# Four moves in a deformable-convolution kernel: first clamp, transpose stores, one input load, and the distances of a chunk

## The chip, the cores and the metric

The kernel runs on one core of a Trainium2 chip. Its engines are TensorE (PE), VectorE (DVE), ScalarE (ACT), GpSimd (POOL) and SyncE (SP), which each work through their own list of instructions and wait for each other by semaphores. The metric is the device time in microseconds (us); the time before is 4453.39 us, the median of three runs (4452.77 to 4454.16).

## What is computed

The input `x` is 8 images of 32 channels and 64 by 64 pixels in float32. It is normalised per image and channel, goes through four blocks and a final layer, and the result is added to `x`:

```python
def _block(x, dc_w, dc_b, of_w, of_b, dw, db):
    h = relu(_deconv2d(x, dc_w, dc_b))           # 3x3
    offset = _conv2d(h, of_w, of_b, PAD)         # 3x3, 18 offsets for each pixel
    return relu(_deform_conv2d(h, offset, dw, db))
in_module = x                                    # the normalised input
x = _block(x, ...0); in_prev = 0
for i in range(1, 4):
    in_cur = x + in_prev
    x = _block(in_cur, ...i)
    in_prev = in_cur
x_cat = concatenate((x, in_module), axis=1)      # 64 channels
offset = _conv2d(x_cat, fin_off_w, fin_off_b, PAD)
return _deform_conv2d(x_cat, offset, fin_dcn_w, fin_dcn_b)
```

`_deform_conv2d` reads each of the 9 taps of a pixel at a place moved by its offsets, with bilinear weights between the four neighbours.

## The kernel before

**Steps.** The work is 5 layers times 2 groups of 4 images, in order: 10 steps, which this text numbers 0 to 9. Steps 0 to 7 belong to the four blocks (a loop `Fori(0, LAYERS)` with both groups in its body), steps 8 and 9 to the final layer. A step has a head and a sampling part. All engines meet at barriers (`clear_step`, `sampling`) between them.

**The head of a step (steps 0 to 7).** PE convolves the input in two units of 32 rows (`conv_tiles`, L516); ACT and DVE write the result to `H` (L828, L994). PE transposes `H` (L531), ACT copies the transposes to the staging tiles `A` (unit 0) and `VT` (unit 1) (`keep_transposes`, L813), and SP stores them to `ht_store` in DRAM (`store_ht`, L371), five DMAs for each unit. PE convolves `H` to the offsets (L516 again). DVE takes them in 8 items of 512 columns: one pass to `FOFF` (L1012) and two reductions for maximum and minimum (L1015, L1016). SP stores each item with two DMAs (`store_offsets`, L379). When the four items of unit 0 have landed, SP loads the offsets of the first two chunks back into `HB`, spread over partitions (`load_offsets`, L389, eight DMAs for each chunk). ACT makes the distances of chunk 0 (`distance`, L730, `DIST`), DVE clamps them (`clamp`, L900), and POOL splits them into two halves of float16, the hats (`hats`: a cast, L1076, then a subtraction, L1078, to `HL`). In the program of DVE the clamp of chunk 0 stands before item 4; in that of POOL `hats(0, 0)` stands before the all-reduce. After item 7 DVE reduces the ranges over columns (to L1035), POOL takes the maximum over partitions (`partition_all_reduce`, L1092), and DVE works out the flags (L1040 to L1062) that choose the shape of the sampling. Then the barrier.

**The sampling.** Each step has 32 chunks of 128 pixels for each of 4 images. The chosen shape is `Shape(0, ...)` (windows of 11 by 11) in steps 0 to 7, and `Shape(1, 2)` (windows of 16 by 16, two batches for each chunk) in steps 8 and 9, as the shapes of the instructions in the trace tell. A chunk has 12 groups g of weights for a batch. For each g PE spreads the y hats and the x hats to the window's positions (L545), ACT copies the y factor out of PSUM (`YC`, L761), and DVE multiplies both to `A` (`one_product`, L895). PE multiplies `A` with the window `VT` (`sample`, L563) for the chunk before in three parts, after g = 4, 7 and 10; ACT reads each part (L740). After g = 1 PE sums the chunk two back over taps (`deform`, L576), ACT reads that (L723) and DVE adds it to the image after product 3 (L889). The y slots in PSUM number 3 and the x slots 4: the spread of y for g waits for the copy of g - 3, that of x for the product of g - 4.

**What the next chunk needs.** While chunk c is worked on, ACT makes the distances of chunk c + 1 (`next_distance`) and DVE clamps them; then POOL makes the hats. Where they stand is set by `next_after`: in shape 0 the distances follow copy 1 and the clamp follows product 2. In shape 1 both follow g = 4 and 5 of the first batch. SP loads the offsets of chunk c + 2 and the windows of chunk c + 1 (L389, L397) in its own loop. The chunk loop (`chunk_loop`) runs two chunks in each of 14 turns, with two chunks in front of it and two behind.

**The final layer** has no first convolution. It needs the normalised input again: SP loads it to `H` at the layer's start (`load_normal(0)`, L354), DVE normalises it (L1001), and PE transposes `X` first and `H` when that is done. Its second group's load is issued in step 8's sampling. `later_loads` also bring the plain input back to `X`.

## Time and profile before

| | us |
|---|---|
| median of three runs | 4453.39 |
| the profiled execution, its own time | 4450.75 |
| its span, first to last instruction | 4448.9 |
| PE busy in it | 3883.5 |
| DVE busy | 3017.8 |
| ACT busy | 2803.3 |
| POOL busy | 1140.5 |
| mean granted clock of TensorE | 0.938 of full speed |

The steps begin some 381 to 387 us apart in steps 0 to 7; steps 8 and 9 take longer. Each instruction stands in the trace with its start and its length. "Idle before" is the time that the engine had nothing to do before it, and behind the arrow stands what ended it; "issue" is idle time that ended without a semaphore that the profile shows. A row of the timeline can hold several instructions in a row (x3); its length is then that of all. PEq, SPq, POOLq and ACTq are the engines' sequencers, which wait, branch, compute addresses and issue DMAs.

### The profile page before, as it was taken

The numbers are of one execution on the slowest core, as the hardware profiler recorded it, in microseconds if no ns is written. First come the engines' busy times: TensorE is split into PE (matmuls) and PEld (weight loads), VectorE is DVE, ScalarE is ACT, GpSimd is POOL, SyncE is SP. The second block draws the span as 40 slices with busy tenths as digits, with TensorE's granted clock in tenths as the row PEclk, the third lists the DMA queues.
The fourth block names the chain that finished last, engine by engine and source line by source line (L and its number), as shares of the span: only waits on it lengthen the run. The fifth ranks groups of instructions, "written<-read, shape, count | busy, mean of one in ns | idle before, by whom it ended". The sixth has DMA issues, their size and how long they took to land.

```text
span 4448.9 us, 221697 instructions
## 1 busy us (share of the span) xinstructions
PE 3883.5 (87%) x81888; PEld 2914.2 (66%) x81888; DVE 3017.8 (68%) x5838; ACT 2803.3 (63%) x6651; POOL 1140.5 (26%) x655
## 2 busy tenths in 40 slices
PE   4998799599879969987986997798699999799998
PEld 3676576477657647765764775576577777577776
DVE  4786588388568738856874884786377776377775
ACT  2786488288558828856873884687155555255554
POOL 0332243033123303413331341332011221012211
PEclk8999899799989979998997998899799999899999
DMA  3442443244244334424433442443666664666664
GB/s 116 122 120 64 122 121 109 75 119 121 62 124 121 102 81 120 122 59 127 120 92 91 121 121 64 121 120 100 172 159 150 150 153 108 170 153 149 153 155 109
DMA packets 243252, 527.18 MB, mean 118 GB/s; under 512 B 61152, under 2 KB 151776, under 8 KB 225632
## 3 DMA queue, kind: packets, MB, share of 16 engines
q1 hardware_dynamic: 242880, 522.27, 45.2%
q8 instruction: 227, 3.72, 0.4%
q14 instruction: 145, 1.19, 0.1%
HBM read 465.57 MB, written 56.45 MB: 117 GB/s over the span
## 4 chain that ended last, share of the span: by engine, by line
PE 49%; issue 17%; DVE 14%; ACT 9%; DMA 3%; SPq 2%; DVEq 2%; ACTq 2%; POOL 1%; POOLq 1%; PEld 0%; PEldq 0%
PE P L545 19%; PE PS L563 19%; DVE A L895 11%; PE P L516 6%; ACT YC L761 5%; PE PS L576 4%; ACT DIST L730 3%; SPq L389 1%; ACT H L828 1%; POOL HL L1078 1%; DMA X<-x_dram 1%; DVEq L927 1%; PE PS L516 1%; DMA HB<-off_store 1%; DVE DIST L900 1%
## 5 line engine op out<-in xcount | busy, mean ns | idle before, releaser
L895 DVE TENSOR_TENSOR A<-P,YC 121x384 f32<-121x384 f32 (+1 forms) x4608 | 2300.1, 549 | 843.5 <-ACT YC L761 627.3
L545 PE MATMUL P<-HL,SEL 32*121 32x384 f16 (+1 forms) x21504 | 1759.7, 304 | 356.7 <-issue 202.2
L761 ACT ACTIVATE YC<-P 121x384 f32<-121x384 f32 (+1 forms) x4608 | 1719.0, 444 | 288.2 <-PE P L545 249.5
L545 PEld LDWEIGHTS P<-HL,SEL 32*121 32x121 f16 (+1 forms) x21504 | 1076.9, 116 | 807.7 <-issue 400.1
L563 PE MATMUL PS<-A,VT 121*32 121x80 f32 (+1 forms) x40960 | 1331.5, 248 | 44.1 <-ACT SMP L740 15.3
L563 PEld LDWEIGHTS PS<-A,VT 121*32 121x32 f32 (+1 forms) x40960 | 1083.3, 116 | 352.8 <-issue 176.5
L1076 POOL CAST HL<-DIST 128x1152 f16<-128x1152 f32 x320 | 366.2, 1144 | 3065.9 <-DVE DIST L900 3065.9
L740 ACT ACTIVATE SMP<-PS 128x480 f32<-128x480 f32 (+3 forms) x1152 | 593.7, 515 | 687.8 <-PE PS L563 682.6
L1078 POOL TENSOR_TENSOR HL<-DIST,HL 128x1152 f16<-128x1152 f32 x320 | 765.9, 2393 | 133.5 <-issue 74.3
L576 PE MATMUL PS<-SMP,CW 128*64 128x128 f32 x7424 | 475.9, 277 | 5.4 <-ACT SMP L740 5.4
L730 ACT ACTIVATE DIST<-HB,CONST 128x1152 f32<-128x1152 f32 x320 | 403.1, 1260 | 103.7 <-DMA HB<-off_store 101.9
L576 PEld LDWEIGHTS PS<-SMP,CW 128*64 128x64 f32 x7424 | 398.7, 137 | 86.6 <-issue 72.5
L889 DVE SCALAR_TENSOR_TENSOR X<-X,CONST,TMP 128x128 f32 (+1 forms) x320 | 280.4, 876 | 79.7 <-ACT TMP L723 79.7
L900 DVE TENSOR_SCALAR DIST<-DIST 128x1152 f32<-128x1152 f32 x320 | 240.2, 751 | 99.1 <-ACT DIST L730 99.1
L516 PE MATMUL P<-X,W 32*32 32x512 f32 x5040 | 208.9, 663 | 89.9 <-POOLq L255 58.2
L516 PEld LDWEIGHTS P<-X,W 32*32 32x32 f32 x5040 | 132.1, 107 | 139.7 <-issue 112.4
L723 ACT ACTIVATE TMP<-PS,BIAS 128x128 f32<-128x128 f32 x320 | 119.0, 372 | 150.2 <-PE PS L576 149.7
L828 ACT ACTIVATE H<-P,BIAS 32x512 f32<-32x512 f32 x128 | 87.8, 686 | 192.5 <-PE P L516 160.6
L516 PE MATMUL P<-H,W 32*32 32x512 f32 x5040 | 207.7, 636 | 1.1 <-issue 1.1
L516 PEld LDWEIGHTS P<-H,W 32*32 32x32 f32 x5040 | 137.6, 105 | 56.5 <-issue 23.1
L994 DVE TENSOR_SCALAR H<-P,BIAS 32x512 f32<-32x512 f32 x96 | 72.0, 750 | 145.2 <-PE P L516 117.8
L1012 DVE SCALAR_TENSOR_TENSOR FOFF<-P,PXB 128x512 f32<-128x512 f32 x70 | 47.8, 683 | 156.6 <-PE PS L516 99.2
(56 smaller groups left out, 667.3 us busy)
## 6 DMA issues: line engine op xcount, KB each, us to landing
HB<-off_store SPq DMA_DIRECT2D x2560, 72.0 KB, 2.4
VT<-ht_store SPq DMA_DIRECT2D x256, 512.0 KB
VT<-ht_store SPq DMA_DIRECT2D x768, 132.0 KB
VT<-ht_store SPq DMA_DIRECT2D x256, 88.0 KB
off_store<-FOFF SPq DMA_DIRECT2D x160, 128.0 KB, 2.6
ht_store<-A SPq DMA_DIRECT2D x32, 256.0 KB, 3.4
ht_store<-VT SPq DMA_DIRECT2D x32, 256.0 KB, 3.6
A<-x_dram SPq DMA_DIRECT2D x2, 2048.0 KB, 10.4
```

Source lines behind the costliest of these rows:

```text
L516: mm = nc.tensor.matmul(bank(bank0 + i)[CH * j:CH * (j + 1), :], weights[q, CH * k:CH * (k + 1)], view(row + k // 3 - 1, col + k % 3 - 1)[ ...
L545: mm = nc.tensor.matmul(dst, SEL[q, table, 0:sh.npos], hats, start=part == 0, stop=part == 1)
L563: mm = nc.tensor.matmul(PS[q:q + wide, sh.unit * v:sh.unit * (v + 1)].rearrange("p (k y x) -> p k y x", k=sh.taps, y=BLK), vt[:, img, :], ...
L576: mm = nc.tensor.matmul(PS[64 * pair:64 * (pair + 1), 0:CPX], CW[:, 64 * k:64 * (k + 1)], rhs, start=k == 0, stop=k == sh.taps - 1)
L730: nc.scalar.activation(DIST[:, :], HB[:, half, :], ACT.Abs, bias=HAT_BIAS).then_inc(abs_done, 1)
L740: nc.scalar.activation(smp_px(0, sh, b * sh.blocks + w, s, count), PS[:, 0:sh.unit * count], ACT.Copy).then_inc(ps_free, 1)
L761: nc.scalar.activation(YC[0:sh.npos, g % X_SLOTS, 0:sh.size], P[0:sh.npos, g % Y_SLOTS, 0:sh.size], ACT.Copy).then_inc(y_ready, 1)
L889: return nc.vector.scalar_tensor_tensor(dst, dst, flag, src, ALU.mult, ALU.add)
L895: return nc.vector.tensor_tensor(dst, x, y, ALU.mult)
L900: nc.vector.tensor_scalar(DIST[:, :], DIST[:, :], SCALE, SCALE, ALU.min, ALU.subtract).then_inc(clamp_done, 1)
L1076: nc.gpsimd.tensor_copy(HL[:, 0, half, :], DIST[:, :]).then_inc(hat_step, 1)
L1078: nc.gpsimd.tensor_tensor(HL[:, 1, half, :], DIST[:, :], HL[:, 0, half, :], ALU.subtract).then_inc(hats_full, 1)
```

## The change

1. **DVE** does the clamp of chunk 0 after the ranges' last operation (L1035), where it waits for the all-reduce, and no longer before item 4.
2. **POOL** does the all-reduce first and the hats of chunk 0 after it.
3. **The stores of the transposes** are issued by ACT, in steps 0 to 7 after each unit's five copies and in steps 8 and 9 after all twenty.
4. **SP** loads the offsets of chunk 0 after unit 0 as before, but those of chunk 1 after all eight items are stored.
5. **The final layer's input** for group 0 is loaded to `H` in the sampling of each block's second group (steps 1, 3, 5 and 7), with a wait for it at the end of SP's sampling; the load at the final layer's start is gone. The first three of the four loads are overwritten by the next layer.
6. **In shape 0** the distances of chunk c + 1 stand in front of copy 0 of chunk c, not behind copy 1, and its clamp stands behind product 1, not product 2. Shape 1 stays as it was.

```diff
-        self.next_after = self.sum_after if self.batches == 1 else self.after[0]
+        self.next_at = 0 if kind == 0 else self.after[0]
@@ SP
                 if final:
-                    load_normal(0)
                     sp.dma_start(CW[:, :], t["fin_dcn_w"]).then_inc(sum_loaded, 16)
@@ SP, step
                 for unit in range(UNITS):
-                    for half in range(UNITS) if final and unit == 0 else [] if final else [unit]:
-                        for n in range(BANKFULS):
-                            store_ht(sources, half, n)
                     for n in range(IMG * unit, IMG * (unit + 1)):
                         store_offsets(n)
                     if unit == 0:
                         for slot in range(OFF_SLOTS):
                             sp.wait_ge(off_stored[slot], 32)
                         load_offsets(0, 0)
-                        load_offsets(0, 1)
+                load_offsets(0, 1)
...
                     if not final and group == GROUPS - 1:
                         load_conv(layer + 1)
+                        load_normal(0)
+                def finish():
+                    if not final and group == GROUPS - 1:
+                        wait_alone(sp, final_loaded, 16 * (layer + 1))
@@ ACT, body
                             n = (c * sh.batches + b) * sh.ngr + g
+                            if sh.kind == 0 and g == sh.next_at and not last:
+                                next_distance(c + 1, band + half, 1 - half)
                             act.wait_ge(y_full, n + 1)
                             act.wait_ge(product_done, n + 1)
                             nc.scalar.activation(YC...).then_inc(y_ready, 1)
-                            if b == 0 and g == sh.next_after and not last:
+                            if sh.kind > 0 and b == 0 and g == sh.next_at and not last:
                                 next_distance(c + 1, band + half, 1 - half)
@@ ACT, step
+                def store_ht(unit, n):
+                    sources = 2 if final else 1
+                    first, count = sheet(unit, n)
+                    width = sources * 128
+                    act.wait_ge(ht_copied, (UNITS * (sources - 1) + unit) * BANKFULS + n + 1)
+                    ...
+                    act.dma_start(dst, staged(sources, unit, n, count)...).then_inc(ht_stored, 16)
...
                     for unit in range(UNITS):
                         keep_transposes(0, unit)
+                        for n in range(BANKFULS):
+                            store_ht(unit, n)
@@ DVE
-                            if b == 0 and g == sh.next_after + 1 and not last:
+                            if b == 0 and g == sh.next_at + 1 and not last:
                                 clamp(c + 1)
...
-                    dve.wait_ge(final_loaded, 16 * (group + 1))
+                    dve.wait_ge(final_loaded, 16 * (LAYERS + group))
...
-                    if n == IMG:
-                        clamp(0)
...
                 flag_count[0] += 1
+                clamp(0)
                 chained()
@@ POOL, step
-                hats(0, 0)
                 pool.wait_ge(flag_step, 4)
                 nc.gpsimd.partition_all_reduce(...).then_inc(flag_step, 1)
+                hats(0, 0)
```

## Rows read from the trace of the kernel before

**Rows 1.** Waits in total: engine line <- what ended them: us, times, longest.

```profile
POOL HL L1078 <- issue: 74.3, 10, 7.9
POOL ST L1092 <- issue: 59.8, 10, 6.7
```

**Rows 2.** Timeline of DVE, head of step 0: start, length, line, idle before.

```profile
90.79 0.76 DVE L900 TENSOR_SCALAR DIST<-DIST 128x1152 f32<-128x1152 f32 x1 [10.16 <-ACT DIST L730]
...
99.69 0.16 DVE L1035 TENSOR_TENSOR ST<-ST,CONST 128x4 f32<-128x4 f32 x1
...
104.29 0.16 DVE L1062 SCALAR_TENSOR_TENSOR FLAG<-ST 128x1 int32<-128x1 f32 x1
```

**Rows 3.** Timeline of PE, step 0: offset convolution's end, chunk 0, chunk 1.

```profile
79.39 3.00 PE L516 MATMUL P<-H,W 32*32 32x512 f32 x68
...
105.79 8.42 PE L545 MATMUL P<-HL,SEL 32*121 32x384 f16 x48 [20.85 <-issue]
121.41 3.65 PE L545 MATMUL P<-HL,SEL 32*121 32x384 f16 x20 [7.21 <-POOL HL L1078]
```

**Rows 4.** Timeline of SP's DMA issues, step 0.

```profile
83.11 7.30 SPq L389 DMA_DIRECT2D HB<-off_store  x16
90.46 3.29 SPq L371 DMA_DIRECT2D ht_store<-VT  x5
93.79 5.76 SPq L379 DMA_DIRECT2D off_store<-FOFF  x8
107.60 9.02 SPq L397 DMA_DIRECT2D VT<-ht_store  x8
116.66 11.97 SPq L389 DMA_DIRECT2D HB<-off_store  x24
```

**Rows 5.** Timeline of POOL, step 0: all-reduce, then chunk 1's subtraction.

```profile
101.79 0.39 POOL L1092 PARTITION_ALL_REDUCE ST<-ST  x1 [6.04 <-issue]
...
118.92 2.35 POOL L1078 TENSOR_TENSOR HL<-DIST,HL 128x1152 f16<-128x1152 f32 x1 [6.95 <-issue]
```

**Rows 6.** Timeline of ACT, step 0: the distances of chunk 2.

```profile
123.38 1.25 ACT L730 ACTIVATE DIST<-HB,CONST 128x1152 f32<-128x1152 f32 x1
```

**Rows 7.** Timeline of SP's DMA issues, step 7.

```profile
2769.47 7.38 SPq L389 DMA_DIRECT2D HB<-off_store  x16
...
2793.57 8.88 SPq L397 DMA_DIRECT2D VT<-ht_store  x8
```

**Rows 8.** Timeline of ACT, step 0: the distances of three later chunks.

```profile
232.04 1.27 ACT L730 ACTIVATE DIST<-HB,CONST 128x1152 f32<-128x1152 f32 x1
...
241.09 1.26 ACT L730 ACTIVATE DIST<-HB,CONST 128x1152 f32<-128x1152 f32 x1
...
250.01 1.27 ACT L730 ACTIVATE DIST<-HB,CONST 128x1152 f32<-128x1152 f32 x1
```

**Rows 9.** Timeline of DVE, a steady chunk: product 2.

```profile
144.12 0.56 DVE L895 TENSOR_TENSOR A<-P,YC 121x384 f32<-121x384 f32 x1 [1.06 <-ACT YC L761]
```

**Rows 10.** Timeline of PE, the same chunk: the x spread of g = 7.

```profile
145.86 0.53 PE L545 MATMUL P<-HL,SEL 32*121 32x384 f16 x2 [0.27 <-DVE A L895]
```

**Rows 11.** Chain of work across the loop's turn: start, us, what.

```profile
149.98 0.04 ACT YC L761
...
150.50 0.06 ACT YC L761
...
150.78 0.04 ACTq L251
...
151.10 0.05 ACTq L251
```

**Rows 12.** Timeline of PE, step 8: the first transposes of H.

```profile
3118.23 1.10 PE L531 MATMUL P<-IDENT,H 128*128 128x128 f32 x4 [8.80 <-DVE H L1001]
```

**Rows 13.** DMA issues of the page: xcount, KB each, median us to landing.

```profile
HB<-off_store SPq DMA_DIRECT2D x2560, 72.0 KB, 2.4
...
H<-x_dram SPq DMA_DIRECT2D x2, 2048.0 KB, 19.4
```

## What I predict

> **What bounds the kernel now.** I read the waits first, then the timelines of one step's head, engine by engine, then the chain across a steady chunk. There are three stretches with different limits.
>
> The **head of steps 0 to 7** is a chain with little overlap. PE ends the offset convolutions at 79.39 + 3.00 = 82.39 [rows 3], so item 4 could be taken then. DVE stands idle for 10.16 us instead, because its next instruction is the clamp of chunk 0, which begins at 90.79 when ACT's distances are done [rows 2]; these need the offsets of chunk 0, whose loads begin at 83.11 [rows 4]. Item 4 follows at about 91.5, the ranges end at 99.69 + 0.16 = 99.85, the flags at 104.45 [rows 2]. PE begins chunk 0 at 105.79 after 20.85 us of idleness, works 8.42 us, and then waits 7.21 us for the hats of chunk 1 [rows 3]: their subtraction starts only 6.95 us after the cast, an idle time that nothing released [rows 5]. This stands in all ten steps (74.3 us in ten waits), as does a similar one before each all-reduce (59.8 us in ten) [rows 1]. I read both as POOL fetching the code of the other function each time that it changes between them.
>
> The **steady chunks of shape 0** take 8.92 us, and 9.05 us across a turn of the loop: the distances start at 232.04, 241.09 and 250.01 [rows 8]. No engine is full. DVE waits 1.06 us for copy 2 [rows 9], which stands behind the distances on ACT, and PE waits 0.27 us for product 3 before its x spread of g = 7 [rows 10]. The ring is: last copy, distances, copy, product 3, spread, part, read of the part, last copy.
>
> **Steps 8 and 9** are bound by PE and keep their chunk loop. Step 8's head has PE waiting 8.80 us for the normalised input [rows 12].
>
> **The sum, part by part**, against the profiled 4450.75 us (2.64 below the median; I add that difference at the end).
>
> *Head of steps 0 to 7.* Without the clamp in front, item 4 starts at 82.4 and the ranges end 99.85 - 9.1 = 90.8 in step 0. The clamp then lies beside the all-reduce (0.76 us against at least 0.39). ACT's five stores of unit 1 cost what SP's did, 3.29 us [rows 4], after copies that follow PE's 82.4 at once; the distances behind them wait for the offsets anyway (83.11 + 3.65 + 2.4 = 89.2 [rows 4, 13]). That cover is nearly used up, and if a store costs more there, the distances and the clamp are late by as much.
>
> Next is late what SP has to do. Its list after 83.11 is eight loads (half of 7.30 = 3.65), eight stores (5.76), and then the eight loads of chunk 1 (3.65), which now stand behind the stores [rows 4]. It comes to the barrier at 83.11 + 3.65 + 5.76 + 3.65 + 0.1 = 96.3. The flags end 104.45 - 101.79 = 2.66 us after the all-reduce's start [rows 2, 5], which I put 0.1 to 1.9 us behind the ranges (the latter as now): at 93.6 to 95.4. So **SP is last at the barrier**. From the flags' end to the first window load it was 107.60 - 104.45 = 3.15 us; so the windows begin at 99.4, which is 8.2 us earlier. The same sum in step 7 gives 24.10 - 16.4 = 7.7 us [rows 7]. I take 8.0 for each of the eight.
>
> Does chunk 1 follow? On POOL the order is now all-reduce, cast, code, subtraction. With the all-reduce's code fetched while POOL idles, it ends at 91.3 to 93.1. To this come cast and gaps (an estimate, 1.6: the cast is the lighter half of the hats), code 7.0, subtraction 2.4 [rows 5] = 11.0 us, against 105.79 - 102.18 = 3.6 us before: the fetch is not gone, it moves from chunk 1 to chunk 0. Chunk 0 starts at 102.3 to 104.1; PE's 8.4 us of it [rows 3] cover the hats of chunk 1, whose subtraction needs no fetch now. So chunk 1 could start at 110.7 to 112.5. Its ACT work begins with the distances of chunk 2, and their offsets land at 116.66 - 8.2 + 3.7 + 2.4 = 114.6 [rows 4, 13]. They start there, 8.7 us before the old 123.38 [rows 6]. Copies 0 and 1 then stand behind them and not in front, some 0.8 us, so copy 2 is 8.0 us early. POOL's path has 2 us to spare. **Eight heads: -64 us**, bounds -52 (a store on ACT at twice its cost, 1.5 us each) and -74 (9.1 us for each, the whole of DVE's gain).
>
> *Steady chunks, steps 0 to 7.* Between the last copy of a chunk and product 3 of the next, ACT and DVE do the same work in either order; only the idle time of DVE moves from product 2 to product 0. I take that at 0 to -0.08 us. But in front of copy 0 stand the sequencer's instructions. Before the distances ACT computes two semaphore values and waits twice: from 150.78 to 151.10 + 0.05 that is 0.37 us [rows 11], now hidden under copies 0 and 1. Across the turn copy 0 starts 150.50 - 149.98 = 0.52 us after the last copy [rows 11], and the 0.13 us more of such a chunk [rows 8] show that this start is in the ring and that within a turn a copy takes 0.39 us. In the new order those 0.39 us cover the sequencer within a turn; across the turn the branch has used that cover already. The distances would start 0.37 us later than that, and all behind them. So 14 turns x 8 steps x (0.37 - 0.09) = +31 us, and -5 us for the other 120 chunks: **+26 us**. Bounds: -19 us, if the sequencer gets ahead (232 chunks x -0.08), and +60 us, if product 0's delay also reaches the part after g = 4.
>
> *Step 8.* DVE has nothing else to do before the input comes, and PE is free 8.80 us before its transposes of H [rows 12]: **-8.8 us**. Those transposes' DMA stores follow on ACT long before anything needs them.
>
> *Steps 8 and 9.* Item 4 waits for PE there, so the clamp gives 0 to -0.6 us. SP comes to the barrier with eight more loads, +0.6 us each; chunk 0's later hats lie under the wait for the input that comes back to X. **+1 us.**
>
> *The four input loads.* 2 MB each, behind the offsets of chunk 3. The two such loads of before took 19.4 us in the median, one of them behind another 2 MB [rows 13]. The next offsets in the queue are needed two chunks later, 18 us. I take **+1 us** in all, bounds 0 and +12 (3 us each). SP's wait for them at the end of the 32 chunks costs nothing.
>
> Sum: -64 + 26 - 8.8 + 1 + 1 = -44.8; profiled 4406, median **4408 us**.
>
> **The rivals.**
> - *The loop does not pay.* The sequencer gets ahead of the branch, or the 0.08 us show. For it: one instruction is usually in the engine's queue ahead. Against it: the 0.13 us of the turn were not hidden. 4408 - 26 - 10 = 4372 us (4360 to 4385).
> - *The all-reduce fetches its code when it is called, not when POOL comes to it.* In this kernel the mechanism would be 6 us behind the ranges instead of the 1.94 us of step 0 (101.79 - 99.85). Chunk 1 would start at 97.2 + 11 + 8.4 = 116.6, two us later than by SP's queue; with the final steps' flags 4 us late that is 8 x 2.5 + 8 = 28 us more: 4436 us. Against it: the all-reduce began 1.94 us after its input was there, so 6 us had not been spent since. The Trainium skill says in GPSIMD Engine Reference, section 2.1, that the first call to a freshly loaded kernel pays some 6 us of loading with no instruction in the profile; by that the reload moves with the first call, and the trace agrees on its size (59.8 / 10) but leaves open when it starts.
> - *Slower: the late product 0 stalls PE.* Product 0 now comes 1.06 us later in the chunk [rows 9], and the x spread of g = 4 and the part behind it wait for it. The part waited for the read of the sum behind the distances anyway, so I estimate that 0.4 us of it arrive there. PE has 0.27 us of idle time behind it [rows 10]. If the spread of g = 7 is pushed back, each 0.1 us costs 23 us; above 0.33 us for each chunk over what I have, it eats everything. With the full 0.4 us, 232 x 0.4 = 93: 4408 - 26 + 93 = 4475 us.
> - *Mixed*: ACT's stores or the loads cost their upper bounds, 4425 to 4440 us.
>
> **How the numbers follow.** Forecast (4390 to 4428) 0.56; no pay in the loop 0.22; mixed 0.09; code at the call 0.07; stall 0.06. The range for 8 in 10 takes in most of the second case and ends above the mixed one: 4368 to 4440. A measurement of this kernel can tell about 0.2% (9 us) from no change, so faster means below 4444.5: 0.89; within 0.2% 0.05; slower 0.06.
>
> **What would show it.** Item 4 at 9 us earlier after item 3, with the ranges' end; SP's eight loads behind the eight stores, and SP as the last at the barrier; the fetch of 7 us before chunk 0's subtraction and none before chunk 1's; the distances of chunk 2 released by their DMA; 9.3 us for a chunk across the loop's turn and 8.9 within it; DVE's idle time of 1 us before product 0; PE without a gap between its transposes of X and H. Wrong would make me: an all-reduce 6 us after the ranges, a DMA wait in chunks 4 and 5 of steps 1, 3, 5 and 7, or a chunk of over 9.3 us in both places.

## The result and the profile after

The changed kernel takes **4395.35 us** in the median of four runs (4392.15 to 4397.59), the kernel before 4453.08 us beside it (4450.37 to 4454.16): a ratio of **0.9871** (95% interval 0.9854 to 0.9888, as behind every ratio below), 57.7 us less. The forecast was 4408 us in a range of 4368 to 4440, so the time came out inside it. The working under it did not hold: its two largest terms were both wrong by over 50 us, and in opposite directions. The profiled execution took 4396.28 us (span 4394.4), 54.5 us less than that of before.

I cut both traces at the same instructions: the first offset item of a step (line 1024, before 1012), the distances of chunks 2, 3 and 31 (line 727, before 730), and the read of the last sum (line 720, before 723). The differences, after minus before, with what the forecast had:

| stretch | forecast, us | measured, us |
|---|---|---|
| heads of steps 0 to 7, first offset item to distances of chunk 3 | -64 | +0.6 |
| chunks 3 to 31 of steps 0 to 7, without the input loads (from e10, below) | +26 | -96.7 |
| the four input loads, in those chunks | +1 | +25.1 |
| between steps 7 and 8 | -8.8 | -10.4 |
| steps 8 and 9: heads +18.2, chunks +3.3 | +1 | +21.5 |
| what comes before the first cut, behind the last chunks, between the other steps | 0 | +5.4 |
| sum | -44.8 | -54.5 |

Up to the distances of chunk 2 the eight heads are 11.0 us shorter together (403.5 to 392.5), up to those of chunk 3 no longer (481.2 to 481.8). Part 6 itself moves these instructions within their chunk; e1, which has parts 1 to 5 without it, gives -6.3 and -0.2 us for the same two cuts.

**The head of step 0.** Timelines of the changed kernel, engine by engine: start, length, engine, line, operation, count, and in brackets the idle time before it with what ended it.

```profile
89.73 0.16 DVE L1047 TENSOR_TENSOR ST<-ST,CONST 128x4 f32<-128x4 f32 x1
...
94.92 0.16 DVE L1075 SCALAR_TENSOR_TENSOR FLAG<-ST 128x1 int32<-128x1 f32 x1
```

```profile
90.03 0.39 POOL L1104 PARTITION_ALL_REDUCE ST<-ST  x1 [84.98 <-DVE ST L1047]
92.26 1.14 POOL L1089 CAST HL<-DIST 128x1152 f16<-128x1152 f32 x1 [1.84 <-DVE DIST L914]
100.74 2.35 POOL L1091 TENSOR_TENSOR HL<-DIST,HL 128x1152 f16<-128x1152 f32 x1 [7.33 <-issue]
107.96 1.14 POOL L1089 CAST HL<-DIST 128x1152 f16<-128x1152 f32 x1 [4.87 <-DVE DIST L914]
109.28 2.37 POOL L1091 TENSOR_TENSOR HL<-DIST,HL 128x1152 f16<-128x1152 f32 x1 [0.18 <-POOL HL L1089]
```

POOL's sequencer at the all-reduce of step 0 (count, shortest/median/longest in ns, start of the first and the last):

```profile
L1104 POOLq MODIFY_POOL_CONFIG  x2: 11/11/11, 32.7 to 32.7; - x2
```

```profile
86.35 7.19 SPq L370 DMA_DIRECT2D off_store<-FOFF  x8
93.58 3.85 SPq L380 DMA_DIRECT2D HB<-off_store  x8
106.23 9.05 SPq L388 DMA_DIRECT2D VT<-ht_store  x8
```

```profile
104.45 9.05 PE L542 MATMUL P<-HL,SEL 32*121 32x384 f16 x60 [20.43 <-issue]
```

```profile
121.30 1.25 ACT L727 ACTIVATE DIST<-HB,CONST 128x1152 f32<-128x1152 f32 x1 [9.38 <-DMA HB<-off_store]
```

DVE has the ranges at 89.89 where it had them at 99.85 [rows 2], and the flags at 95.08. The all-reduce starts 0.14 us behind the ranges; its change of configuration stood at 32.7, long before its input. That the 7.33 us ahead of the subtraction are the loading of code is my reading: the trace shows the idle time and the change of configuration before it, not the loading itself. SP has issued its last load before the barrier at 97.43, and then issues nothing until 106.23; before, the windows began at 107.60 [rows 4]. PE starts chunk 0 at 104.45, where it was 105.79 [rows 3]. Of the 9.4 us gained at the flags, 1.3 arrive; and since this step began 0.8 us earlier (its first offset item at 72.08, before at 72.89), only 0.5 of them are the head's. The one engine that is busy in between is POOL: its subtraction for chunk 0 ends at 100.74 + 2.35 = 103.09, and PE follows 1.4 us later. SP's wait at the barrier (L253) ends at 103.19, and its first window follows after 3.0 us of its own reads and address work.

**The steady chunks.** First two groups of the page's part 5 (before, then after): busy us and mean ns, then the idle time ahead. It is the update of X by the sum of the chunk two back, which I call the residual; it stands on DVE behind product 3.

```profile
L889 DVE SCALAR_TENSOR_TENSOR X<-X,CONST,TMP 128x128 f32 (+1 forms) x320 | 280.4, 876 | 79.7 <-ACT TMP L723 79.7
```

```profile
L903 DVE SCALAR_TENSOR_TENSOR X<-X,CONST,TMP 128x128 f32 (+1 forms) x320 | 172.2, 538 | 79.7 <-ACT TMP L720 79.7
```

The same instruction on the same data is 338 ns shorter in the mean, 108 us in all. Beside it stands POOL's cast of the hats. DVE and POOL in one chunk of before, then in one of after:

```profile
226.66 1.08 DVE L889 SCALAR_TENSOR_TENSOR X<-X,CONST,TMP 128x128 f32 x1
```

```profile
226.44 1.14 POOL L1076 CAST HL<-DIST 128x1152 f16<-128x1152 f32 x1 [5.30 <-DVE DIST L900]
```

```profile
221.80 0.61 DVE L903 SCALAR_TENSOR_TENSOR X<-X,CONST,TMP 128x128 f32 x1
```

```profile
221.12 1.14 POOL L1089 CAST HL<-DIST 128x1152 f16<-128x1152 f32 x1 [4.97 <-DVE DIST L914]
```

Before, the cast begins 0.22 us ahead of the residual, ends at 227.58, and the residual at 227.74. After, the distances stand two copies earlier in ACT's list and the clamp one product earlier in DVE's, and the cast begins 0.68 us ahead of the residual; it ends at 222.26, the residual at 222.41. In both the residual ends 0.15 us behind the cast, however long it has run, and so it does in all 232 such chunks of each execution (0.14 to 0.16). A chunk takes 8.58 us in the mean of steps 0, 2, 4 and 6 (8.98 before), and its chain has only PE in it. The line of shares above the chain of waits of 203 to 230 us of after:

```profile
by line: PE P L542 54.2%; PE PS L560 32.8%; PE PS L573 13.8%
```

The turn of the loop costs 8.70 - 8.47 = 0.23 us, before 0.13 [rows 8].

**The input loads.** In steps 1, 3, 5 and 7 the mean chunk is 8.79 us and not 8.58. SP's issues in step 1 of after:

```profile
492.43 0.66 SPq L355 DMA_DIRECT2D H<-x_dram  x1
493.46 14.93 SPq L380 DMA_DIRECT2D HB<-off_store  x8
...
531.62 4.01 SPq L380 DMA_DIRECT2D HB<-off_store  x8
535.98 3.93 SPq L388 DMA_DIRECT2D VT<-ht_store  x4
540.57 3.84 SPq L380 DMA_DIRECT2D HB<-off_store  x8
544.79 3.95 SPq L388 DMA_DIRECT2D VT<-ht_store  x4
549.00 4.00 SPq L380 DMA_DIRECT2D HB<-off_store  x8
```

The eight small loads behind the 2 MB copy take 14.93 us to issue, against 4 us. Afterwards SP has no pause left: a turn of two chunks from 531.62 to 549.00 is 17.38 us of issuing one after the other, and PE would need 8.47 + 8.70 = 17.17, or 17.09 as in step 1 of e10. So the lost time isn't made up until the end of the step. In step 0 SP issues one after the other too, but its turn takes 222.59 - 205.49 = 17.10 us, a little less than PE's:

```profile
205.49 3.84 SPq L380 DMA_DIRECT2D HB<-off_store  x8
...
222.59 3.84 SPq L380 DMA_DIRECT2D HB<-off_store  x8
```

So in the even steps SP stays ahead; in the odd ones it lives on the lead it has at the start, which the copy takes away. Why its turn is longer there is open. The waits of after have, for PE's wait for windows (us, times, longest):

```profile
PE PS L560 <- DMA VT<-ht_store: 31.7, 49, 1.9
```

### The profile page after: what moved, and what is told of

Read it like the earlier page. It is cut to its first block, busy times and chain, and to the rows that moved or that the text cites. A ratio compares the mean times of both kernels' runs of the same rounds, so it can differ in the third digit from the quotient of the medians.

```text
span 4394.4 us, 221688 instructions
## 1 busy us (share of the span) xinstructions
PE 3849.4 (88%) x81888; PEld 2958.5 (67%) x81888; DVE 2931.0 (67%) x5838; ACT 2782.9 (63%) x6651; POOL 1145.0 (26%) x655
## 4 chain that ended last, share of the span: by engine, by line
PE 61%; SPq 21%; issue 7%; DMA 3%; POOLq 3%; ACT 2%; DVE 2%; POOL 0%; ACTq 0%; DVEq 0%; PEld 0%; PEldq 0%
PE P L542 22%; PE PS L560 22%; SPq L388 10%; SPq L380 10%; PE P L513 7%; PE PS L573 7%; POOLq L256 2%; ACT H L840 1%; PE PS L513 1%; DMA X<-x_dram 1%; DMA HB<-off_store 1%; PE P L528 1%; DVE FOFF L1024 1%; DMA off_store<-FOFF 0%; DVE ST L1028 0%
## 5 line engine op out<-in xcount | busy, mean ns | idle before, releaser
L542 PE MATMUL P<-HL,SEL 32*121 32x384 f16 (+1 forms) x21504 | 1730.0, 303 | 323.1 <-issue 216.2
L542 PEld LDWEIGHTS P<-HL,SEL 32*121 32x121 f16 (+1 forms) x21504 | 1124.0, 116 | 697.1 <-issue 351.6
L903 DVE SCALAR_TENSOR_TENSOR X<-X,CONST,TMP 128x128 f32 (+1 forms) x320 | 172.2, 538 | 79.7 <-ACT TMP L720 79.7
```

The costliest lines, as they stand in the source:

```text
L542: mm = nc.tensor.matmul(dst, SEL[q, table, 0:sh.npos], hats, start=part == 0, stop=part == 1)
```

## The experiments

My theories by then: **port**, that the residual is held while POOL's cast or subtraction runs, and the new order only moves it; **barrier**, that POOL's own arrival is last since its hats stand ahead of it; **loads**, that a copy on SP costs what SP can't make up. Their rival throughout is the prediction's own working.

### e1: the order of the distances put back

```diff
-        self.next_at = 0 if kind == 0 else self.after[0]
+        self.next_at = self.sum_after if kind == 0 else self.after[0]
...
-                            if sh.kind == 0 and g == sh.next_at and not last:
-                                next_distance(c + 1, band + half, 1 - half)
                             act.wait_ge(y_full, n + 1)
...
-                            if sh.kind > 0 and b == 0 and g == sh.next_at and not last:
+                            if b == 0 and g == sh.next_at and not last:
                                 next_distance(c + 1, band + half, 1 - half)
```

> The changed kernel with part 6 undone: distances of the next chunk behind copy 1, clamp behind product 2, all else as changed. Theory of the port: the residual on VectorE (1.08 us before in 232 chunks, 0.61 us after) stands still until GpSimd's cast of the hats has ended, and part 6 only moved that cast earlier. So the residual is back at 1.08 us, a steady chunk at 8.9 to 9.05 us, and the kernel takes about 4395 + 68 = 4463 us, a little over the kernel before. Theory of the prediction: the order costs 26 us by the sequencer's waits across the loop's turn, so undoing it gives 4395 - 26 = 4369 us.

Measured **4460.91 us** (4455.79 to 4474.72, ten runs), ratio 1.0024 (1.0013 to 1.0035). The residual's mean is back:

```profile
L901 DVE SCALAR_TENSOR_TENSOR X<-X,CONST,TMP 128x128 f32 (+1 forms) x320 | 280.2, 876 | 79.7 <-ACT TMP L720 79.7
```

All that the change gives comes from part 6; parts 1 to 5 by themselves make the kernel some 8 us slower. The loop's term of +26 is out.

### e2: the order of the distances alone, in the kernel before

The edit is the counterpart of e1.

```diff
-        self.next_after = self.sum_after if self.batches == 1 else self.after[0]
+        self.next_at = 0 if kind == 0 else self.after[0]
...
+                            if sh.kind == 0 and g == sh.next_at and not last:
+                                next_distance(c + 1, band + half, 1 - half)
...
-                            if b == 0 and g == sh.next_after + 1 and not last:
+                            if b == 0 and g == sh.next_at + 1 and not last:
                                 clamp(c + 1)
```

> The kernel before with part 6 alone. Theory of the port: residual 0.61 us, steady chunks 8.47 and 8.70 us in all eight steps of shape 0, since no input load stands in SP's queue: 8 x 11.3 = 90 us less, 4363 us, which is under the changed kernel. If the second groups stay at 8.9 us a chunk instead, the load was not what slowed them, and it is 4381 us. Theory of the prediction: 4453 + 26 = 4479 us.

Measured **4365.01 us** (4361.4 to 4367.06), ratio 0.9803 (0.9787 to 0.982). Part 6 alone is worth 88 us, 30 more than the whole change. The two halves aren't additive: +7.8 and -88.1 give -80.3, and the change has -57.7. The input loads are one reason: with chunks of about 9 us (e1) they add 1.5 us a step to the 28 chunks (9.077 us a chunk against 9.023), with chunks of 8.6 us some 6.

### e3: the residual moved, the distances left where they were

```diff
-                            if before >= sh.lag and b == sh.batches - 1 and g == sh.sum_after + 2:
+                            if before >= sh.lag and b == sh.batches - 1 and g == sh.sum_after + (2 if sh.kind else 4):
```

> The kernel before with one edit: in shape 0 the residual follows product 5 and not product 3; the distances stay behind copy 1. Theory of the port: the cast has ended by then, the residual takes 0.35 us, and the chunk falls to about PE's own pace, 8.5 us or less: 4453 - 232 x 0.45 = 4349 us, with nothing moved on ScalarE. It could stop short of that where GpSimd's subtraction holds the port as the cast did: then the residual is longer than before (up to 2.4 us) and the kernel slower, 4453 to 4700 us. Theory that the gain is the order on ScalarE (the stall of VectorE moved from product 2 to product 0): no change, 4453 us.

Measured **4390.64 us** (4385.77 to 4398.24), ratio 0.9862 (0.9845 to 0.9879). The group of the residual, and DVE's timeline over a chunk:

```profile
L889 DVE SCALAR_TENSOR_TENSOR X<-X,CONST,TMP 128x128 f32 (+1 forms) x320 | 109.8, 343 | 79.7 <-ACT TMP L723 79.7
```

```profile
212.07 0.56 DVE L895 TENSOR_TENSOR A<-P,YC 121x384 f32<-121x384 f32 x1 [1.05 <-ACT YC L761]
...
214.61 0.34 DVE L889 SCALAR_TENSOR_TENSOR X<-X,CONST,TMP 128x128 f32 x1
...
220.80 0.56 DVE L895 TENSOR_TENSOR A<-P,YC 121x384 f32<-121x384 f32 x1 [1.10 <-ACT YC L761]
```

POOL in the same chunk:

```profile
213.46 1.14 POOL L1076 CAST HL<-DIST 128x1152 f16<-128x1152 f32 x1 [4.92 <-DVE DIST L900]
214.79 2.42 POOL L1078 TENSOR_TENSOR HL<-DIST,HL 128x1152 f16<-128x1152 f32 x1 [0.18 <-POOL HL L1076]
```

This shows the residual's part without touching ACT: two products later it begins as POOL's cast ends (214.60) and takes 0.34 us; the record of the subtraction begins 0.16 us before it is over. The size was missed. I had 4349 us, as if the whole length were on the path. The chunk fell from 8.98 to 8.70 us, not to the 8.58 of the changed kernel. DVE still waits 1.05 us for copy 2, as in [rows 9]. Part 6 frees less of the residual (0.47 us against 0.74) and gains more (88 us against 62), so it must open something besides; that this is the ring over ACT's distances is argued, and no run sets the two shares apart.

### e8: the same two products later in the changed kernel

The edit is that of e3, in the changed kernel.

> The changed kernel with the edit of e3: the residual after product 5. Theory of the port: in the new order the cast has ended then, but GpSimd's subtraction (2.4 us) has begun about 0.2 us before, so the residual stands still until that ends, 2 us or more for each of 232 chunks; the stall falls in PE's cover only in part, so 1 us a chunk: 4395 + 230 = 4600 us. Theory that a residual further back in the chunk is better in itself (e3 was 62 us faster): 4395 us or less.

Measured **4761.54 us** (4757.0 to 4771.08), ratio 1.069 (1.067 to 1.071). The group, then DVE and POOL in one chunk:

```profile
L903 DVE SCALAR_TENSOR_TENSOR X<-X,CONST,TMP 128x128 f32 (+1 forms) x320 | 434.3, 1357 | 79.7 <-ACT TMP L720 79.7
```

```profile
231.69 2.06 DVE L903 SCALAR_TENSOR_TENSOR X<-X,CONST,TMP 128x128 f32 x1
```

```profile
231.21 2.38 POOL L1091 TENSOR_TENSOR HL<-DIST,HL 128x1152 f16<-128x1152 f32 x1 [0.18 <-POOL HL L1089]
```

The same shift that gained 62 us in the kernel before costs 366 us here; a part of it is TensorE's clock, whose mean granted value was 0.903 in the profiled execution against 0.934. POOL stands earlier in the chunk, so the residual now meets the subtraction: that ends at 233.59, the residual at 233.75, again 0.16 us behind it. So it goes in 144 of the 232 chunks; in the others the residual comes later in the subtraction and takes 0.91 us or more, and in all 232 it ends 0.14 to 0.16 us behind it. The sign was as the port theory has it, and a residual that is merely late on the path can't take 2.06 us; of the size I had little more than half. The mean residual of the 232 chunks is 1.13 us longer than in the changed kernel (1.74 against 0.61) and the chunk 1.7 us longer (10.27 against 8.58 in the even steps); the rest I take for what the products behind it hold up on PE and ACT, and for the clock, which no run sets apart. The Trainium skill has a rule for this in SBUF — State Buffer, section "Who interferes with whom": the port pair that DVE shares with GpSimd is an exclusive lock, a DVE instruction with two inputs in SBUF contends with a GpSimd instruction that reads SBUF, and the order of issue decides who blocks. The trace agrees where GpSimd is first: the residual reads X and TMP, both in SBUF, and is held for 0.74, 0.27 and, in most chunks of e8, 1.72 us beyond its 0.34; the products, with one input in PSUM, keep their 0.55 us throughout. GpSimd held by the residual, the other order, no run here shows.

### e4: POOL arrives at the barrier ahead of its hats

```diff
-                hats(0, 0)
-                sampling(pool, bar_count, final, body_of, lambda sh: None, clears=True)
+                sampling(pool, bar_count, final, body_of, lambda sh: None, clears=True, between=lambda: hats(0, 0))
...
-            barrier(eng, bar_count)
+            if between is None:
+                barrier(eng, bar_count)
+            else:
+                eng.drain().then_inc(bar, 1)
+                between()
+                wait_alone(eng, bar, 5 * (bar_count + 1))
```

A wait for the hats in ACT's fallback path, which doesn't run here, is left out above.

> The changed kernel, but GpSimd signals its arrival at the barrier right behind the all-reduce, then makes chunk 0's hats, then waits for the barrier. Theory of the barrier: the head gained almost nothing because the barrier waits for the 11 us of hats and code on GpSimd, so the window loads begin at 106.23 us in step 0. Now SP is last (97.7), the windows begin at 101, the distances of chunk 2 at 116 instead of 121.3: 8 x 4.9 less, and 6 and 10 us less in steps 8 and 9: 4395 - 55 = 4340 us. Rival: the hats of chunk 0 themselves bound the head, wherever the barrier is: within 5 us of 4395 us.

Measured **4340.5 us** (4337.33 to 4343.59), ratio 0.9745 (0.9729 to 0.9761). POOL and SP in the head of step 0:

```profile
101.74 2.35 POOL L1097 TENSOR_TENSOR HL<-DIST,HL 128x1152 f16<-128x1152 f32 x1 [7.01 <-issue]
```

```profile
96.33 3.85 SPq L385 DMA_DIRECT2D HB<-off_store  x8
103.67 9.39 SPq L393 DMA_DIRECT2D VT<-ht_store  x8
```

SP now issues the windows at 103.67, before POOL's subtraction has ended (104.09), and 3.5 us after its own last load (100.18): it is the last one, as I had forecast for the change itself. (Step 0 begins 2.4 us later in this execution, with its first offset item at 74.49, so that its times don't compare directly with those above.) The time from the first offset item to the distances of chunk 2 falls from 49.1 us to 44.1 in steps 0 to 7 (50.4 before), in steps 8 and 9 from 73.9 and 78.9 us to 67.1 and 70.2. All ten together give 55.6 us, and the time fell by 54.9. Up to the distances of chunk 3 the ten heads give 50.6, and the chunks behind them 4.7.

### e5: the old order of clamp and hats in the changed kernel

```diff
                     unit, image = divmod(n, IMG)
+                    if n == IMG:
+                        clamp(0)
...
-                clamp(0)
...
+                hats(0, 0)
                 pool.wait_ge(flag_step, 4)
...
-                hats(0, 0)
```

> The changed kernel with parts 1 and 2 undone: the clamp of chunk 0 before item 4 again, the hats of chunk 0 before the all-reduce; stores on ScalarE, the loads of chunk 1 behind the stores and the rest stay. Theory of the barrier (GpSimd's hats and the 7 us of code stand in front of it since the change): item 4 is 9 us late again, but the barrier passes at once; steps 0 to 7 lose about 1 us each and steps 8 and 9 win back their 6 and 10 us: 4395 + 8 - 16 = 4387 us. Theory of the prediction (parts 1 and 2 are worth 8 us in each of eight heads): 4395 + 64 = 4459 us.

Measured **4386.34 us** (4385.51 to 4394.31), ratio 0.9851 (0.9835 to 0.9868): 9 us less with parts 1 and 2 undone, though the single runs of the two kernels just overlap. As they stand they gain 1.0 us in each of eight heads up to chunk 2, and lose 7.3 and 7.8 us in steps 8 and 9. There the distances are ready long before the ranges, so the hats and POOL's wait of 7 us used to be over by then, and now stand behind the all-reduce and ahead of the barrier.

### e6: the input load behind the last windows

```diff
                         load_conv(layer + 1)
-
-                        load_normal(0)
...
                     if not final and group == GROUPS - 1:
-
+                        load_normal(0)
                         wait_alone(sp, final_loaded, 16 * (layer + 1))
```

> The changed kernel with one line moved: the final layer's input is loaded behind the last windows of SP's list and not behind the offsets of chunk 3. Theory of the queue: the 2 MB load delays the next offsets and windows, and since SP's turn of 16.8 us fills the 17.2 us of two chunks, SP never makes it up; with it gone the second groups (245 to 247 us from chunk 3 to 31) fall to the 240.1 us of the first groups: 4395 - 4 x 6 = 4371 us, and 2 us less for chunks 2 and 3. Rival: the second groups are slow for another reason, such as the address registers or the weights' load in front of it: 4395 us.

Measured **4380.63 us** (4379.97 to 4384.02), ratio 0.9835 (0.9819 to 0.9852). That is 10 us above my 4371. The chunks gave back 25.0 us as expected (2937.9 to 2912.9 in all ten steps), but the stretch behind chunk 31's distances grew by 16.2 us in the sum of ten. Step 7, table by windows: from:to, length, busy us and count of PE, PEld, DVE, ACT, POOL, then the granted clock, the share of the DMA engines and GB/s.

```profile
2998.00:3005.00 7.00, 6.93 (x188) 5.13 (x181) 5.28 (x11) 5.68 (x14) 0.00 (x0) 1.00 0.72 172
3005.00:3009.00 4.00, 1.37 (x53) 1.02 (x53) 0.35 (x1) 0.94 (x2) 0.00 (x0) 0.91 1.04 224
3009.00:3013.00 4.00, 2.74 (x72) 2.48 (x75) 0.00 (x0) 0.57 (x1) 0.00 (x0) 0.50 0.46 98
```

```profile
3009.51 1.81 PE L558 MATMUL PS<-A,VT 121*32 121x80 f32 x43 [1.78 <-issue]
```

While the copy has the DMA engines to itself, PE stands still for 1.78 us in the middle of a run of equal matmuls, with nothing that released it, and then works at half its clock (0.50, that is 1.2 GHz; it had been busy for 1.37 of the 4 us before). Such a stall stands at the same place in each of the four steps with the copy (1.27, 1.55, 1.36 and 1.78 us) and in none of the others. What PE waited for there the trace doesn't say. One trace record points at its instructions: the second DMA packet of the instruction queue q8 in this stretch starts 18.4 to 18.9 us behind chunk 31's distances in the four steps with the copy, and 13.4 to 14.1 us in step 0 and in the same four steps of e10. That this is the cause is not shown.

### e10: the input load back in step 8's head

```diff
                 if final:
+                    load_normal(0)
                     sp.dma_start(CW[:, :], t["fin_dcn_w"]).then_inc(sum_loaded, 16)
...
                         load_conv(layer + 1)
-
-                        load_normal(0)
...
-                    if not final and group == GROUPS - 1:
-
-                        wait_alone(sp, final_loaded, 16 * (layer + 1))
+                    pass
...
-                    dve.wait_ge(final_loaded, 16 * (LAYERS + group))
+                    dve.wait_ge(final_loaded, 16 * (group + 1))
```

This undoes part 5 of the list of changes, which the text below calls part 3.

> Edit: the new kernel with its part 3 alone undone: the last layer's first input is loaded at the head of step 8 again, no input is loaded in steps 1, 3, 5 and 7, and SP's wait at their end is gone. If the copies in those steps cost what the chunks of steps 1, 3, 5 and 7 have over those of the even steps (about 25 us by their sums of chunks, part of it in the copy itself and part in SP, whose turn of 16.8 us hardly catches up in one of 17.2), and step 8's head gains about 10 us by the load ahead (49.95 to 39.58 us), the time is about 4395 - 25 + 10 = 4380 us. If they cost the 1 us of the forecast's sum and step 8's head is worth 8.8 us, it is about 4395 - 1 + 9 = 4403 us. In the trace: chunks of 8.62 and 8.47 us in steps 1, 3, 5 and 7 by the first, still above 8.7 us in the mean by the second.

Measured **4367.13 us** (4366.17 to 4374.47), ratio 0.9815 (0.9799 to 0.9832). The early input loads cost 28 us in all. Chunks 3 to 31 of steps 1, 3, 5 and 7 lose 25.5 us against the changed kernel, those of step 9 lose 3.1, and step 8 pays 10.6 us for it. It gained 13 us more than I had put down; the larger part of these is in the heads of steps 5, 7 and 9, which are 11.2 us shorter together. SP's issues in step 1, and PE's waits for windows:

```profile
493.44 0.38 SPq L347 DMA_DIRECT2D W<-conv_w_dram  x1
494.18 4.93 SPq L381 DMA_DIRECT2D HB<-off_store  x8
```

```profile
PE PS L557 <- DMA VT<-ht_store: 1.7, 4, 0.6
```

### e7, e9 and e11: what the findings give together

e7 is e4 and e6 in one; e9 is e7 with the residual behind product 10, where POOL is through; e11 is e9 with the input load as in e10.

> Both: GpSimd signals its arrival before the hats of chunk 0, and the final layer's input is loaded behind the last windows. If the two costs are apart from each other: 4340.5 - 26 = 4314 us. If the head's gain came from the slack that the late load leaves, less than that: 4340 us.

e7: **4335.8 us** (4327.04 to 4341.36), ratio 0.9726 (0.9709 to 0.9742). A miss by 22 us. 11 us of it are e6's, of which I had taken 26 and which gave 14.7: by what e4 and e6 measured, 4340.5 - 14.7 = 4326 was to be had. The other 10 us no run explains. The profiled execution is the slowest of the four and shows two chunks of 9.86 and 11.17 us in step 1 and two of 18.86 and 19.16 in step 9; such pairs come at chunks 3 to 6 in several kernels. The input load isn't needed for them (step 7 of e6 has 10.15 and 11.53 us with no load in front of them); what makes them is open.

```diff
-                            if before >= sh.lag and b == sh.batches - 1 and g == sh.sum_after + 2:
+                            if before >= sh.lag and b == sh.batches - 1 and g == sh.sum_after + (2 if sh.kind else 9):
```

> Edit: the version with GpSimd's arrival ahead of its hats and the input load behind the last windows (4335.8 us), and in the chunks of steps 0 to 7 VectorE's residual behind product 10 in place of product 3, where GpSimd's cast and subtraction for the chunk have both ended. By the theory that GpSimd's operations hold the residual, it takes its free 0.34 us there (0.61 behind product 3, 2.06 behind product 5 in this order); TensorE bounds the chunk, so the mean chunk of 8.58 us may fall by 0 to 0.1 us, and the time is 4310 to 4336 us. If the residual's length is set by something that follows it (the buffers that it reads, ACT's copies), it stays at 0.6 us or more and the time at 4336 us or above.

e9: **4307.72 us** (4304.1 to 4318.38), ratio 0.9684 (0.9668 to 0.9701). The group of the residual, DVE and POOL in one chunk, and PE's waits for windows:

```profile
L907 DVE SCALAR_TENSOR_TENSOR X<-X,CONST,TMP 128x128 f32 (+1 forms) x320 | 110.1, 344 | 91.4 <-ACT TMP L723 91.4
```

```profile
211.81 0.34 DVE L907 SCALAR_TENSOR_TENSOR X<-X,CONST,TMP 128x128 f32 x1
```

```profile
207.03 1.14 POOL L1093 CAST HL<-DIST 128x1152 f16<-128x1152 f32 x1 [4.58 <-DVE DIST L918]
208.35 2.42 POOL L1095 TENSOR_TENSOR HL<-DIST,HL 128x1152 f16<-128x1152 f32 x1 [0.18 <-POOL HL L1093]
```

```profile
PE PS L563 <- DMA VT<-ht_store: 13.4, 23, 1.1
```

The residual is at its free length, and the gain of 28 us is 2 more than the top of what I gave it. Even steps take 8.44 us a chunk, the odd ones 8.54, and there PE waits for windows again without any input load in the middle. SP's turn is the next bound: it takes 17.35 us in step 1, where PE needs 8.33 + 8.48 = 16.81. e11, with no input load in these steps at all, has the same waits (14.3 us in 27).

> Edit: the version with GpSimd's arrival ahead of its hats and the residual behind product 10 (4307.7 us), with the last layer's first input loaded at the head of step 8, as in the kernel before, in place of behind the last windows of steps 1, 3, 5 and 7. By the theory that a 2 MB copy costs wherever SP has it in a step that TensorE bounds, since SP's own turn has no time to spare, this is worth what it was in the new kernel, where the copy at the end gave 4380.6 us and the load in step 8's head 4367.1 us: about 13 us, so 4290 to 4300 us. If the copy is free behind the last windows, the head of step 8 gets 10 us longer and nothing comes back: about 4318 us.

e11: **4297.48 us** (4296.37 to 4300.19), ratio **0.9655** (0.9639 to 0.9671), the fastest of all and 98 us under the changed kernel.

## Why the prediction was right, and where it wasn't

The time fell into the range, but that was luck: two errors of over 50 us cancelled, and the gain came from a stretch in which the working had a loss. By its steps:

- *Item 4 some 9 us earlier, with the ranges' end.* Right: the ranges end at 89.89, where 90.8 was forecast. *The all-reduce 0.1 to 1.9 us behind them.* Right, 0.14; the rival that puts 6 us between the ranges and the all-reduce is out. *The fetch moves from chunk 1 to chunk 0.* Right, as far as its place and length go: 7.33 us ahead of chunk 0's subtraction, 0.18 ahead of chunk 1's.
- *"So SP is last at the barrier."* **Wrong, the first failed step.** SP came at 97.43 (forecast 96.3). But hats(0, 0) had been moved behind the all-reduce, so POOL had cast, fetch and subtraction in front of its own arrival: 103.09. I had worked out POOL's order and its time (102.3 to 104.1 for chunk 0), and used it for chunk 0's start alone; that every engine's arrival stands behind its own queue I asked of SP only. Windows at 106.23 and not 99.4, distances of chunk 2 at 121.30 and not 114.6. They were released by their DMA, as forecast; the eight heads gave 11 us up to chunk 2 and nothing up to chunk 3, where -64 was put down. e4 removes just this and gets 55 us, of steps 0 to 7 5.0 each, so that against the kernel before a head is 6.4 us shorter up to chunk 2 and 4.2 up to chunk 3, where 8.0 was forecast. So the barrier is most of this miss and not all. SP's eight stores of unit 1 were a term too small besides: 5.76 us were put down, and they took 6.0 to 8.6 us in steps 0 to 7 (7.19 in step 0), the first of them issued beside ACT's stores.
- *"Between the last copy of a chunk and product 3 of the next, ACT and DVE do the same work in either order."* **Wrong, the second failed step.** I took the residual's 1.08 us as fixed. Most of its length was a wait for POOL, hidden in a busy time, and it depends on when the cast starts. The ring of rows 9 and 10 opened, and the bound is PE. -96.7 us stand where +26 was put, outside the bounds of -19 and +60. The sequencer's 0.37 us did show at the turn, with 0.10 us more than before, not 0.28. My rival of a loop that does not pay had the sign, at a tenth of the size; the slower rival is out, as PE has no stall to wait in.
- *Input loads +1, bounds 0 and +12.* **The size failed**: +25.1 in the chunks. I had costed the copy by what it holds up at once, and compared the next need (18 us) with its 19.4. What I left out is that SP issues for 17.4 us in each turn of 17.2 in these steps and can't catch up, and that this slack depends on the chunk's length, which I believed to stay at 9 us.
- *Step 8's head -8.8*: right, -10.4; e10 pays 10.6 for undoing it.
- *Steps 8 and 9 +1*: +21.5, mostly from the failed step of the barrier: e5 with the old order gets 15.7 us of it back in the heads, e4 16.2. e10, without the early input loads, is 9.3 us better there as well, which I can't place.
- *Slips of the working* that change nothing: the head's lower bound is 8 x 9.1 = 73 us and not 74; the 0.09 in the turn's term (0.37 - 0.09) stands on no row; the limit of 0.33 us for each chunk is 71 / 232 = 0.31; and 4406 + 2.64 rounds to 4409.

So the errors are +65 us in the heads, +24 in the loads and +20 in steps 8 and 9, against -123 in the chunks. A forecast may be close to the time and be worth nothing as an explanation; here e1 and e2 show it, since by the prediction part 6 alone cost 26 us, and it gained 88.

Open are the pairs of long chunks at chunks 3 to 6, the 3 us of step 9, the shares of the residual and of ACT's ring in the 88 us of part 6, and the head times of steps 5, 7 and 9 that hang on the input load.

## What to carry to other kernels

When an instruction's mean differs between places in one profile, lay the other engines' timeline beside it: a duration can hold a wait, and then moving either engine's work changes both. At a barrier, list for every engine what is queued ahead of its own arrival, the waits at a change of function included; let an engine arrive first and do its preparatory work between arrival and wait. Before a large copy goes into a loop, add up the issuing queue's own turn against the loop's, at the length that the loop has after the change.

## What the runs showed that I had not expected

- The residual takes 0.34 us where POOL stands still, 0.61 and 1.08 beside its cast, 0.91 to 2.08 beside its subtraction, and ends 0.14 to 0.16 us behind POOL's instruction in each case. The cast keeps its 1.14 us and the subtraction its 2.4.
- The all-reduce began 0.14 us behind its input when POOL had stood idle for 85 us before it, while the first subtraction behind it waited 7.33 us. So whatever its change of configuration (at 32.7) costs was over before its input came.
- Eight loads of 72 KB take SP 3.9 us to issue in every chunk, and 14.93 us when they stand behind one copy of 2 MB.
- In e6 TensorE stood still for 1.27 to 1.78 us inside a run of matmuls in each of the four steps with a late 2 MB copy; in step 7 the DMA engines' share was 1.04 beside it, and the granted clock 0.50 behind it.
